# First attention: outputs turned on VectorE in 32 by 32 blocks and divided on GpSimd, with the heads of an item four apart

## The reference

```python
x = x + linear_attention(layernorm(x))      # the "first attention"
x = x + experts(layernorm(x))               # 16 experts, 4 of them chosen per token, and 2 shared ones
x = x + softmax_attention(layernorm(x))     # the "second attention"
x = x + experts(layernorm(x))               # the same weights again
```

```python
phi_q, phi_k = elu(x @ Wq.T) + 1, elu(x @ Wk.T) + 1;  v = x @ Wv.T
num[t] = sum over s <= t of (phi_q[t] . phi_k[s]) * v[s]     # per head
den[t] = sum over s <= t of (phi_q[t] . phi_k[s]) + 1e-5
out = (num / den) @ Wo.T + bo
```

## Time and profile before

| what | value |
|---|---|
| median of 3 timed runs | 549.83 us (549.31 to 550.15) |
| the profiled execution, its own time | 547.0 us |
| its span, first to last instruction | 545.2 us |
| granted TensorE clock over the span | 0.999 of full |
| first attention, slots 7 to 35 | about 27 to 96 us of the span |
| experts' stage, first matmul of unit 0 | 96.05 us |

### The profile page before, as it was taken

One profiled execution on the slowest core, in us unless ns is written; L12 is line 12 of the kernel. 1 busy time (PEld: TensorE's weight loads), 2 busy tenths in 40 slices (PEclk: granted clock), 3 DMA queues, 4 the chain that ended last, 5 costly groups with the idle time before them and its releaser, 6 DMA issues. The chain is left out here.

```text
span 545.2 us, 11779 instructions
## 1 busy us (share of the span) xinstructions
PE 508.4 (93%) x3789; PEld 387.8 (71%) x3789; DVE 414.7 (76%) x1113; ACT 336.5 (62%) x598; POOL 332.5 (61%) x423
## 2 busy tenths in 40 slices
PE   6888989999999999999888988989989999999997
PEld 5665656777888888887645655645778888888885
DVE  4677798599798796577877887998588786786665
ACT  3777766566555555756568677676765555555553
POOL 5897583588777877767332142140577776776563
PEclk9999999999999999999999999999999999999999
DMA  6477780355355454581632434110354364565351
GB/s 174 128 263 226 236 259 3 104 111 93 112 131 92 121 127 121 120 227 47 230 118 97 137 113 139 61 40 2 101 97 110 100 137 106 124 145 109 105 148 44
DMA packets 67254, 67.60 MB, mean 124 GB/s; under 512 B 9073, under 2 KB 54146, under 8 KB 67202
## 3 DMA queue, kind: packets, MB, share of 16 engines
q1 hardware_dynamic: 64096, 66.47, 46.3%
q10 hardware_dynamic: 3106, 0.48, 0.5%
HBM read 53.56 MB, written 13.37 MB: 123 GB/s over the span
## 5 line engine op out<-in xcount | busy, mean ns | idle before, releaser
L794 POOL TENSOR_TENSOR KS<-PT,QS 128x512 fp32r<-128x512 f32 x143 | 184.9, 1294 | 78.8 <-ACT QS L1034 72.8
L1029 ACT ACTIVATE bank<-bank 128x512 f32<-128x512 f32 x128 | 74.6, 583 | 94.9 <-PE bank L1058 94.3
L1756 DVE TENSOR_TENSOR PT<-CS,bank 128x512 f32<-128x512 f32 x128 | 87.6, 684 | 50.4 <-PE bank L1058 43.7
L1056 PE MATMUL bank<-XH,WH 128*128 128x512 f32 (+1 forms) x288 | 114.6, 398 | 0.0
L1058 PE MATMUL bank<-XH,WL 128*128 128x512 f32 (+1 forms) x288 | 112.3, 390 | 0.0
L1057 PE MATMUL bank<-XL,WH 128*128 128x512 f32 (+1 forms) x288 | 112.2, 389 | 0.0
L1034 ACT ACTIVATE QS<-PT 128x512 fp32r<-128x512 f32 x144 | 90.1, 626 | 15.0 <-DVE PT L1761 14.9
L1761 DVE TENSOR_TENSOR PT<-PT,bank 128x512 f32<-128x512 f32 x128 | 88.1, 688 | 8.0
L1640 DVE TENSOR_REDUCE MEXP<-bank 128x4 f32<-128x1024 f32 x64 | 78.3, 1223 | 18.3 <-PE bank L1178 17.9
L936 ACT ACTIVATE PT<-bank 128x1024 f32<-128x1024 f32 x64 | 65.4, 1026 | 36.1 <-PE bank L1212 35.4
L1235 PE MATMUL bank<-PT,V 128*32 128x256 f32 (+1 forms) x1024 | 61.7, 358 | 0.7 <-ACT OTS L950 0.7
(11 more groups left out here) (209 smaller groups left out, 784.2 us busy)
## 6 DMA issues: line engine op xcount, KB each, us to landing
CS<-combine_rows SPq DMA_DIRECT2D x128, 256.0 KB, 4.8
head_rows<-HP SPq DMA_DIRECT2D x28, 256.0 KB, 3.1
QS<-head_rows SPq DMA_DIRECT2D x28, 256.0 KB, 2.8
KS<-head_rows SPq DMA_DIRECT2D x28, 256.0 KB, 3.1
head_rows<-PHI SPq DMA_DIRECT2D x14, 256.0 KB, 3.6
stage<-in_L_ffn_gate_w_dram SPq DMA_DIRECT2D x5, 192.0 KB, 3.5
stage<-in_L_ffn_up_w_dram SPq DMA_DIRECT2D x5, 192.0 KB, 3.9
stage<-in_L_ffn_down_w_dram SPq DMA_DIRECT2D x5, 192.0 KB, 4.8
```

The lines of the kernel that those rows point to most:

```text
L794: pool.tensor_tensor(GL[:, (u - 1) % 3, :], GG[:, (u - 1) % 3, :], GH[:, (u - 1) % 3, :].bitcast(f32), ALU.subtract).then_inc(F.gl, 1)
L1029: act.activation(TH[:, u, :] if u < SHARED else G[u % 3][:, :], G[u % 3][:, :], ACT.Silu).then_inc(F.th, 1)
L1056: pe.matmul(out, wh, vh, start=start, stop=False)
L1756: dve.tensor_tensor(ab, CS[:, e % CBUFS, :], U[u % 3][:, :], ALU.mult).then_inc(F.b, 1)
```

## The change

In the first attention (k = 0) the outputs no longer pass PE. DVE turns `OTS` in 32 by 32 blocks into a new tile `OTD` (128x512), and takes the reciprocals from there: 64 for each partition, one to a block. POOL multiplies `OTD` with them into `OTOK`, with the heads placed so that DVE can turn the whole of `OTOK` back in 32 by 32 blocks into `OTT`, every eighth slot. The heads of an item are four apart in all chunks, so the read of `head_rows` has another pattern. PE's `output_turn` and its turning of `OTOK`, and ACT's copy to `OTT`, are for the second attention only. Some waits move along with that. Apart from that, `CBT` is written to DRAM in two DMAs in place of four, for both stages of experts.

The diff, cut to what the text speaks of:

```diff
 SP, first_rows
-      spread[w, c % 2, HG * j:HG * (j + 1)].rearrange("h s c t -> (h s c) t"))
+      spread[w, c % 2].rearrange("(h j) s c t -> j h (s c) t", j=HG)[j])
 SP, rows
-      for i in range(4):
-          sp.dma_start(combine[k, c].rearrange("b (j i a) -> i b j a", j=2, i=4)[i],
-                       CBT[32 * i:32 * (i + 1), :].rearrange("b (j a) -> b j a", j=2)).then_inc(F.cr, 16)
+      for j in range(2):
+          sp.dma_start(combine[k, c].rearrange("b (j i a) -> j i b a", j=2, i=4)[j],
+                       CBT[:, 32 * j:32 * (j + 1)]).then_inc(F.cr, 16)
 POOL, slot (behind the addition of bo, ahead of the experts' layer norm)
+      q = (n - 7) // 2
+      if k == 0 and n % 2 and 0 <= q < PAIRS:
+          pool.wait_ge(A.rd, q + 1)
+          if q % HG == 0 and q:
+              pool.wait_ge(A.ott, q // HG)
+          pool.tensor_tensor(OTOK[:, :, :].rearrange("p t (b j v) -> p (t b) j v", b=4, j=HG)[:, :, q % HG, :],
+                             OTD[:, :].rearrange("p (b r) -> p b r", r=32)[:, :, 0:HD],
+                             RDEN[:, :, :].rearrange("p t h -> p (t h)").unsqueeze(2).broadcast_to([P, 4 * CT, HD]),
+                             ALU.mult).then_inc(A.nm, 1)
 ACT, slot
-      if n >= 14 and g == 6 and c - 1 < CHUNKS:
+      if k == 1 and n >= 14 and g == 6 and c - 1 < CHUNKS:
 PE, output_turn
-      if n % 2 == 0 or not 0 <= q < PAIRS:
+      if k == 0 or n % 2 == 0 or not 0 <= q < PAIRS:
 PE, side_steps (n = 14, 22, 30, 38)
-      if n >= 14 and g == 6 and c - 1 < CHUNKS:
+      if k == 1 and n >= 14 and g == 6 and c - 1 < CHUNKS:
 DVE, normalised
+      if k == 0:
+          dve.wait_ge(A.ot, q + 1)
+          if q:
+              dve.wait_ge(A.nm, q)
+          dve.transpose(OTD[:, :], OTS[:, :]).then_inc(A.nt, 1)
+          dve.wait_ge(A.nt, q + 1)
+          dve.reciprocal(RDEN[:, :, :].rearrange("p t h -> p (t h)"),
+                         OTD[:, :].rearrange("p (b r) -> p b r", r=32)[:, :, HD]).then_inc(A.rd, 1)
+          return
 DVE, side_steps
+      if k == 0 and n >= 14 and g == 6 and c - 1 < CHUNKS:
+          dve.wait_ge(A.nm, HG * c)
+          ...
+          dve.transpose(OTT[:, :], OTOK[:, :, :].rearrange("p t d -> p (t d)")).then_inc(A.ott, 1)
```

More of the change, by code:

```diff
@@ L158, in hybrid_block @@
         OTOK = sb("OTOK", [P, CT, DM])
+        OTD = sb("OTD", [P, CHUNK])
         OTT = sb("OTT", [P, CHUNK])
@@ L439, in first_rows @@
                         sp.dma_start(t[:, j, :].bitcast(f32),
-                                     spread[w, c % 2, HG * j:HG * (j + 1)].rearrange("h s c t -> (h s c) t"))\
+                                     spread[w, c % 2].rearrange("(h j) s c t -> j h (s c) t", j=HG)[j])\
                           .then_inc(A.qr[j], 16)
@@ L480, in rows @@
                 sp.wait_ge(A.cb, c + 1)
[L481 to L484 removed]
+                for j in range(2):
+                    sp.dma_start(combine[k, c].rearrange("b (j i a) -> j i b a", j=2, i=4)[j],
+                                 CBT[:, 32 * j:32 * (j + 1)]).then_inc(F.cr, 16)
+                sp.wait_ge(F.cr, 32 * (c + 1))
                 for e in range(EXPERTS):
@@ L1235, in values_product @@
                             m = pe.matmul(OT[32 * h:32 * (h + 1), SEQ * b + q0:SEQ * (b + 1)],
-                                          V[:, cc % 2, 2 * b + kt, HG * h + j if k == 0 and cc == 0 else HG * j + h, :], src,
+                                          V[:, cc % 2, 2 * b + kt, HG * h + j if k == 0 else HG * j + h, :], src,
                                           start=(kt == 0), stop=(kt == 1), skip_group_check=True)
@@ L1247, in output_turn @@
                         pe.wait_ge(A.nm, q)
-                    elif k == 1:
+                    else:
                         pe.wait_ge(FF[0].res, CHUNKS)
-                    if k == 1 and q == 2:
+                    if q == 2:
                         pe.wait_ge(LN[2].xs, CHUNKS)
[L1252 to L1255, removed]
                     if g == 7 and c:
@@ L1279, in side_steps @@
                             pe.wait_ge(s_w1, 1)
+                        elif n == 8:
+                            pe.wait_ge(s_cd, 4)
                         else:
-                            pe.wait_ge(A.nm, (n - 6) // 2)
+                            pe.wait_ge(L.xl, NORM0_TURN[n])
                         first_turn(NORM0_TURN[n])
@@ L1294, in side_steps @@
                         pe.wait_ge(A.ott, c - 1)
-                        if c <= CHUNKS:
+                        if k == 0 and c == 2:
+                            pe.wait_ge(L.xl, CHUNKS)
+                        elif k == 0:
+                            pe.wait_ge(Lnext.xs, min(c - 2, 2))
+                        elif c <= CHUNKS:
                             pe.wait_ge(A.nm, HG * (c - 1) + 1)
-                        elif k == 1:
+                        else:
                             pe.wait_ge(A.th, 2)
@@ L1304, in side_steps @@
                         pe.wait_ge(Lnext.xn, 2 * (NORM_TURN[k][n] + 1))
-                        if n < ITEMS:
+                        if k == 1 and n < ITEMS:
                             pe.wait_ge(A.nm, HG * (c - 1) + 3)
+                        elif k == 0 and n < ITEMS:
+                            pe.wait_ge(A.res, c - 1)
                         elif NORM_TURN[k][n] < CHUNKS - 1:
@@ L1665, in normalised @@
                         dve.wait_ge(A.e1, cc)
[L1666 to L1669, removed]
+                    tok = OTOK[:, :, 32 * j:32 * (j + 1)].rearrange("p t (h c) -> p t h c", h=4)
                     dve.tensor_tensor(tok, o[:, :, :, 0:HD], RDEN[:, :, :].unsqueeze(3).broadcast_to([P, CT, 4, HD]),
@@ L1680, in side_steps @@
                 def side_steps():
+                    if k == 0 and n >= 14 and g == 6 and c - 1 < CHUNKS:
+                        dve.wait_ge(A.nm, HG * c)
+                        if c >= 2:
+                            dve.wait_ge(A.e2, c - 1)
+                        else:
+                            dve.wait_ge(s_qkl, 1)
+                        dve.transpose(OTT[:, :], OTOK[:, :, :].rearrange("p t d -> p (t d)")).then_inc(A.ott, 1)
                     if n >= 16 and g == 0 and c - 2 < CHUNKS:
@@ L1728, in slot @@
                     if n == WEIGHTS_SLOT[k]:
-                        dve.wait_ge(FF[0].cr, 64 * CHUNKS)
+                        dve.wait_ge(FF[0].cr, 32 * CHUNKS)
                         combine_rows_turned(A, 0)
@@ L1795, in unit @@
                     if u == WEIGHTS_UNIT[prev]:
-                        dve.wait_ge(F.cr, 64 * (c + 1))
+                        dve.wait_ge(F.cr, 32 * (c + 1))
                         combine_rows_turned(AT[k], c + 1)
```

## The result

The changed kernel takes 578.44 us (median of 4 runs, 576.88 to 579.6); the kernel before, beside it, 549.57 us (548.11 to 550.15). The ratio is 1.0533, with a 95% interval of 1.0509 to 1.0558: slower by 28.9 us, where the prediction had +10 and ended its range at 566 us. The profiled execution took 578.41 us, its span 576.6.

The account below looks back on a forecast made before the run. It took a ring of waits through DVE, ACT and PE as the bound. The first attention's +8.5 us and the experts' +1.5 us made +10.0 us: 559.8 us forecast, with 552.5 to 566 us for 8 in 10.

Parts of the forecast that it names:

- the ring: First attention: DVE's masks, ACT's copy and PE's products wait for each other in turn, 1.71 us a round, setting the order.
- The turn: First attention, DVE: turning OTS (128x512) in blocks for each pair was priced at 0.70 us.
- The reciprocal: First attention, DVE: the new reciprocal of each pair, taken as 128x64, was priced at 0.53 us.
- the division: First attention, POOL: multiplying a pair's 128x512 outputs with the reciprocals was priced at 1.1 us.
- The holds on POOL: DVE's turn of OTOK in slots 14 and 22 waits 2.4 us for POOL's division; charged +2.55 and +1.8 us.
- Slots 7 to 21: First attention: DVE's added work is mostly hidden; 0.7 us for slots 7 to 13, 0.35 us for 15 to 21.
- Slots 23 to 34: First attention: routing and stats keep DVE busy; six odd slots at 0.65 us, less 0.2 us of PE waits: 3.7 us.
- The experts' start: The product with Wo before unit 4 waits for a turn on DVE: +2.9 us there, +1.5 us net.
- POOL is never late: Rival: POOL runs ahead enough in slots 13 and 21, the two holds of 2.4 us go: 555 us; chance 0.14.
- The DVE work is dearer: Rival: DVE's turn grows like 1.89 us or slows beside POOL, some 17 us more: 576 us; chance 0.07.
- PE is the bound after all: Rival: taking turns off PE lets DVE's idle time fill up, a gain: 543.5 to 548 us; chance 0.08.

Follow-up runs that it names:

- e2: The kernel before, with only the reads of an item's heads four apart (values and output places put in that order): 579.89 us, ratio 1.0555.
- e1: The changed kernel with rows read as before, four neighbouring heads in one transfer, and rows of Wo permuted to match: 556.96 us, ratio 1.0169.
- e4: e1 with POOL's division moved to the head of its slot, ahead of the split of the next weights: 557.82 us, ratio 1.0129.
- e15: e4 with the last turn back of OTOK put ahead of the expert unit's multiplication that waits for combine rows: 551.95 us, ratio 1.0063.
- e9: The kernel before, with each read taking eight rows from each of the 16 heads, as many bytes: 550.30 us, ratio 1.0033.
- e3: The changed kernel with each read of four heads cut into four transfers of one head: 570.29 us, ratio 1.0376.

## Why the prediction was wrong

**The step that failed** is the sentence "The read's new pattern moves the same rows; I cost it at nothing." It counted bytes and looked only at when the read is issued. The read alone costs 31.4 us (e2). Its bytes move at a quarter to a third of the rate, over four of 16 engines by the shares above; PE waits 17.3 us for rows in the stage, and the queue that it holds delays the weights, whose wait of 6.87 us stops the ring again. The diff showed the four parts, and no rival weighed them. The page of the Trainium skill named above has the rule. The trace of before could not have shown it for these rows, since every read of them there was one list of 128.

**The clock** stood in no term. The earlier trace rows show 1.00 for the whole stage, and the prediction let PE have less to do as if that were free. In e1, with quick reads, the windows show 0.74 to 0.91 from 27 to 107 us.

**The turn**, 0.70 us: right, 702 ns. **The reciprocal**, 0.53 us, and **the division**, 1.1 us: mis-sized, 0.25 and 0.41 us. The blocks are 32 columns wide, so 512 columns hold 16 denominators and 128 outputs for each partition; the text ahead took 64 and 512, and a view of the same size stood in the earlier trace rows (249 ns for 128x16). **The holds on POOL** are where they were forecast, in slots 14 and 22, released by the division, with 1.67 and 1.68 us for 2.4; the 0.7 us between are the division's error. But taking them out (e4) gains nothing that can be told, where +2.55 and +1.8 us had been charged. **Slots 7 to 21** were to cost 1.05 us beside the holds; e15 is level at slot 20. **Slots 23 to 34**, 3.7 us at 0.65 us for each of six odd slots: the mechanism was right, and the size 0.42 us where e15 shows it, the error being mostly the reciprocal's. **The experts' start**: a wait of almost 4 us before the product with Wo; 1.66 us in the changed kernel, 2.64 us in e4, and moving the turn takes it away. The experts' first matmul came at 127.46, not 104.5.

**The sum** of these terms, +10.0 us, is near to the +8.5 us of e1, which leaves the read out; but that is half chance, since terms that came out smaller were made up by a clock that the sum did not have.

**Rivals.** "POOL is never late" fails: it was late. "The DVE work is dearer" has a time near the one measured (576) and the wrong cause: the turn is not dearer. "PE is the bound after all" fails: no run of the changed order is faster than before; up to slot 20, at full clock, the ring is level with before without PE's turns (e15), so there they had been hidden.

## What to carry to other kernels

Before a transfer's pattern is changed, look at its outermost count, not only at its bytes: four parts moved at 105 GB/s and two at 52, while with one list of 128 rows (e1) or sixteen parts (e9) the engines were 0.7 to 0.9 busy and moved some 200 to 400 GB/s. An in-order queue turns one slow transfer into late transfers for everyone behind it, so price the queue, not the transfer. Work taken off an engine that is not the bound may still cost time, where that engine's clock falls when it stands: in e15 a values product took 1.51 us in place of 0.86.

## What the runs showed of the hardware

- A read of 256 KB in four parts kept 26.1% of the 16 DMA engines' time busy, one in two parts 13.1%, each engine at work moving 24 GB/s.
- An issue on SP took 0.43 to 0.6 us for 64 KB as for 256 KB (e3: 1.82 us for four), so cutting a transfer in four costs SP about four times the issue time.
- With several reads outstanding, an issue lasted as long as a read took to move: 2.44 us with four parts, 5.00 with two.
- A turn in 32 by 32 blocks took 702 ns for 128x512 in fp32 and 236 ns for 128x64, also beside POOL's work.
- The granted clock fell to half after PE had stood for a us or more (in e15 to 0.50 from 67 to 73 us, after 1.16 us), but not after each such wait: e15 kept 1.00 from 79 to 81 us with PE busy 0.68 of 2.00 us. The runs don't settle what decides it.

```profile
79.00:81.00 2.00, 0.68 (x12) 1.00 0.72 250
```
